# Transformer layer on one core: even tile's scores ahead of the odd tile's transposes in three early steps, with new orders for the downward products, the last output blocks and the second routing product

## The chip, the cores and the metric

The kernel runs on one core of a Trainium2 chip. The metric is the device time of one execution in microseconds (us). A measurement of this kernel tells a change from none at about 0.2%, some 2.3 us.

## The reference

One pre-norm transformer layer over x of 8 batches x 512 tokens x 256 features, all float32:

```python
x = x + attention(layernorm(x))   # rms norm with gamma, 16 heads of 64, softmax(q k^T / 8) v, w_out
x = x + ffn(layernorm(x))         # gelu(x w1 + b1) w2 + b2, 256 -> 1024 -> 256
# the ffn result is scaled by the sum of the two renormalised top router
# probabilities of 8 experts
```

## The kernel before

Every float32 operand of a product is split in two parts, hi (the value rounded to fp32r) and lo (the rest), and a product is three matmuls: hi with hi, lo with hi, hi with lo. ScalarE (ACT) or GpSimd (POOL) writes the hi part and VectorE (DVE) the lo part, from the matmul's result in PSUM. All engines walk lists written out by hand, in the order of the code; semaphores tie them together. TensorE (PE) takes its weight loads and matmuls from one list too.

**Attention.** A tile n is 128 queries of a pair of heads; there are 256 tiles, four to a pair (`NUNIT`). The loop goes over steps -10 to 129, two tiles to a step. PE does in step s: the 64x64 transposes of the probabilities of the odd tile 2s-3 (`transpose_prob`, recorded at L681, 32 in all), the scores of tiles 2s and 2s+1 (`scores`, L642 and L648, six matmuls for each), the transposes of the even tile 2s-2, then projection blocks (`aux`, its products at L615: in steps 3, 5 and 7 the one block of v; in even steps q and k of a coming pair; from step 8 on output blocks too), and in odd steps the weighted values of a pair (`weighted_values`, L696, 16 matmuls). In step 127 the scores of tile 254 already precede the transposes of tile 251.

What is waited for around the change:

- `scores(n)` waits for both exponentials of tile n-2 (`exp`, ACT L980), whose bank it writes.
- `transpose_prob` of the odd tile 2s-3 in an odd step waits until DVE has the lo part of tile 2s-4 (`transposed_lo`, DVE L1204, `s_ptlo`); that of the even tile 2s-2 in an odd step waits for the lo part of the keys projected in the step before (`aux_done` of k, DVE L1204, `nat`).
- `aux` of a block at place 1, as the v block of steps 3, 5 and 7, waits for the first half of the lo part of the odd tile 2s-3: `pe.wait_ge(s_ptlo, 2 * tile + (1 if place == 1 else 2))`.
- DVE does in an odd step: the reciprocal of tile 2s-1, the lo part of the late keys, `transposed_lo(2s-3)` in two halves, `row_max(2s)` (L1288), `transposed_lo(2s-2)`, `row_max(2s+1)`.

**The seam.** Steps 128 and 129 also hold the first four upward products of the feed-forward part (`up`, L615, six matmuls of 512 columns for each). The lo part of the last attention-side input, `input_lo(8)`, is done by DVE at the end of step 127; `up(0, 0)` waits for it. Step 128 has two output blocks of 12 matmuls each, out(30, 0) and out(30, 1).

**Feed-forward.** For each batch c: eight `up` blocks, gelu on ACT (L995), hi part on POOL (L1084), lo part on DVE (L1204), then `down` for four tiles of 128 tokens. In `down`, each of eight slices f of the hidden features is one matmul of 512 columns (hidden hi with both parts of w2, L856, last L860) and one of 256 (hidden lo with w2 hi, L857, last L859), alternating; the last tile of batch 7 is three matmuls of 256 columns a slice. Tile 0 waits for the lo part of each slice (`s_hlo`). In batch 0, after two tiles, come the last two output blocks (`last_outs`, 24 matmuls, waiting for the last pair's attention output from POOL, L1112) and then `route(1)`, the router's product for batch 1 (L824, four matmuls of 512 columns). `up(c, f)` waits for the gelu two blocks before, and that, from the fourth on, for the lo part three blocks before.

Of the kernel before, what the change touches and what calls it, by code (L numbers as in the profile page):

```python
# [31 lines left out]
P = 128  # L32
B, SEQ, D = 8, 512, 256
# [6 lines left out]
FT = FF // P  # L40
# [3 lines left out]
NUNIT = 2 * NHEAD  # L44
# [12 lines left out]
STEPS = NUNIT // 2  # L57
# [4 lines left out]
TAIL_UPS = 4  # L62
# [9 lines left out]

PS_UP = (0, 1)
PS_ROUTER = 2
PS_DOWN = (5, 6, 4, 7)
PS_LAST_OUT = (3, 1)

# [58 lines left out]
def layer_kernel(nc, x, gamma_cols, w_qkv, w_out, router_w, w1, b1_cols, w2, b2_rows, ident, out):  # L136
# [13 lines left out]
    with ExitStack() as ctx:  # L150
# [6 lines left out]
        ps = ctx.enter_context(nc.psum_tensor("ps", [P, 8, 512], F32))  # L157
# [7 lines left out]
        w2_both = wbig_parts[:, :, KT * FF:KT * FF + FT * D].rearrange("p i (k n) -> p k i n", k=FT)  # L165
# [51 lines left out]
        def hidden(part, f):  # L217

            assert (STEPS - 2) % NHALF == 0
            place = 2 * (f % TT)  # L220
            return pT[part][:, 0 if f >= TT else 2, place:place + 2, :].rearrange("p k q -> p (k q)")
# [106 lines left out]
        def down_bank(c, tile):  # L328
            return PS_DOWN[tile]

        def by_parts(c, tile):

            return c < B - 1 or tile < TT - 1
# [276 lines left out]
        def _(pe):  # L610
            def products(dst, stationary, moving, first, last):

                terms = [(0, 0), (1, 0), (0, 1)]
                for n, (i, j) in enumerate(terms):
                    ins = pe.matmul(dst, stationary[i], moving[j], start=first and n == 0,  # L615
                                    stop=last and n == len(terms) - 1)
                return ins
# [211 lines left out]
            def up(c, f):  # L829
                n = c * FT + f  # L830
                if n == 0:
                    wait_x2_split(0)
                    wait_weight_split(pe, 9)
                    pe.wait_ge(s_exp, 2 * NUNIT - 2)
                if n >= 2:
                    pe.wait_ge(s_gelu, n - 1)
                if n == FT + 1:
                    pe.wait_ge(s_added, len(out_tasks))
                for k in range(KT):
                    ins = products(ps[:, PS_UP[n % 2], :], [w[:, k, f * P:(f + 1) * P] for w in w1s],  # L840
                                   [v[c % 2][:, k, :] for v in f_xT], k == 0, k == KT - 1)
                ins.then_inc(s_up, 1)

            def down(c, tile):
                part, t = divmod(tile, 2)
                if c >= 1 and t == 0:
                    pe.wait_ge(s_fo, 2 * (c - 1) + part + 1)
                for f in range(FT):
                    if tile == 0:
                        pe.wait_ge(s_hlo, c * FT + f + 1)  # L850
                    bank = ps[:, down_bank(c, tile), :]
                    tokens = [hidden(i, f)[:, tile * P:(tile + 1) * P] for i in range(2)]
                    if not by_parts(c, tile):
                        ins = products(bank[:, 0:D], tokens, [w[:, f, :] for w in w2s], f == 0, f == FT - 1)
                    elif f < FT - 1:
                        pe.matmul(bank, tokens[0], w2_both[:, f], start=f == 0, stop=False)  # L856
                        pe.matmul(bank[:, 0:D], tokens[1], w2s[0][:, f, :], start=False, stop=False)  # L857
                    else:
                        pe.matmul(bank[:, 0:D], tokens[1], w2s[0][:, f, :], start=False, stop=False)  # L859
                        ins = pe.matmul(bank, tokens[0], w2_both[:, f], start=False, stop=True)  # L860
                if t == 1 or tile == TT - 2 and c == B - 1:
                    ins.then_inc(s_down, 1)

# [1 line left out]
                for n in range(count):  # L865
                    pe.matmul(ps[:, PS_SCORE[1], :], pT[0][:, 0, 0, 0:P], pT[0][:, 0, 0:2, :], start=True, stop=True)

            SCORE_TILES = {1: (4,), 2: (5,), STEPS - 1: (NUNIT - 1,)}

            pe.wait_ge(s_warm, 1)  # L870
            for step in range(FIRST_STEP, LAST_STEP + 1):
                keep_warm(WARM.get(step, 0))
                first, rest = aux_of(step)
                tail = 2 * step - UP_SLOT
                if step == STEPS - 1:
                    scores(2 * step)
                if 0 <= 2 * step - 3 < NUNIT:
                    transpose_prob(2 * step - 3)
                for n in SCORE_TILES.get(step, (2 * step, 2 * step + 1)):
                    if 0 <= n < NUNIT:  # L880
                        scores(n)
                if 0 <= 2 * step - 2 < NUNIT and step != 1:
                    transpose_prob(2 * step - 2)
                if 0 <= tail < TAIL_UPS:
                    up(0, tail)
                for block_of_aux in first:
                    if block_of_aux[1:3] == (2, "out") and first[-1][2] == "k":
                        begin_keys(step, *first[-1])
                    aux(step, *block_of_aux)
                if step == LAST_STEP:  # L890
                    up(0, tail + 1)
                if pair_at(step) is not None:
                    weighted_values(pair_at(step))
                for block_of_aux in rest:
                    aux(step, *block_of_aux)
                    if step == 0 and block_of_aux[2] == "k":
                        scores(2)
                        transpose_prob(0)
                    if step == 0 and block_of_aux[2:] == ("v", 0, 0):
                        scores(3)  # L900
                if 0 <= tail < TAIL_UPS and step < LAST_STEP:
                    up(0, tail + 1)

            route(0)
            for c in range(B):
                for f in range(TAIL_UPS if c == 0 else 0, FT):
                    up(c, f)
                if 1 <= c < B - 1:
                    route(c + 1)
                if c == 0:  # L910
                    wait_weight_split(pe, N_CHUNKS - 1)
                    pe.wait_ge(s_added, added_no(NPAIR // 2 - 2, 1))
                    pe.wait_ge(s_halves, STEPS)
                down(c, 0)
                down(c, 1)
                if c == 0:
                    last_outs()
                    route(1)
                down(c, 2)
                down(c, 3)  # L920

# [245 lines left out]
        def _(dve):  # L1167
# [185 lines left out]
            for step in range(FIRST_STEP, LAST_STEP + 2):  # L1353
                if 0 <= 2 * step - 1 < NUNIT and step < STEPS - 1:
                    row_inverse(2 * step - 1)
                if step == 1:
                    row_max(2)
                    aux_done(*late_blocks(0)[0])
                    row_max(3)
                    row_inverse(2)  # L1360
                    for block_of_aux in late_blocks(0)[1:]:
                        aux_done(*block_of_aux)
                    transposed_lo(0)
                else:
                    for block_of_aux in late_blocks(step - 1):
                        aux_done(*block_of_aux)
                    if 0 <= 2 * step - 1 < NUNIT and step >= STEPS - 1:
                        row_inverse(2 * step - 1)
                    if step == STEPS - 1:
                        row_max(2 * step)  # L1370
                    if 0 <= 2 * step - 3 < NUNIT:
                        transposed_lo(2 * step - 3)
                    if 0 <= 2 * step < NUNIT and step < STEPS - 1:
                        row_max(2 * step)
                    if step % 2 == 0 and 0 <= 2 * step + 1 < NUNIT:
                        row_max(2 * step + 1)
                    if 0 <= 2 * step - 2 < NUNIT:
                        transposed_lo(2 * step - 2)
                    if step % 2 and 0 <= 2 * step + 1 < NUNIT:
                        row_max(2 * step + 1)  # L1380
                    if 0 <= 2 * step < NUNIT:
                        row_inverse(2 * step)
                for block_of_aux in sorted(early_blocks(step), key=lambda block: block[1:3] != (2, "out")):
                    aux_done(*block_of_aux)
                slot_tasks(2 * step)
                slot_tasks(2 * step + 1)
                for block_of_aux in turned_blocks(step):
                    aux_done(*block_of_aux)
                if split_step(step) and split_step(step) < B:
                    input_lo(split_step(step))  # L1390
                if step == STEPS - 1:
                    input_lo(B)

            def turn_logits(c):

# [126 lines left out]
```

## Time and profile before

| | |
|---|---|
| median of 3 runs | 1161.59 us (1160.44 to 1162.55) |
| the profiled execution | 1160.57 us, span 1158.8 us |
| PE busy | 1146.5 us (99%) |
| DVE busy | 1008.1 us (87%) |
| ACT busy | 875.0 us (76%) |
| POOL busy | 664.9 us (57%) |
| granted TensorE clock | 1.00 in every stretch that was read |

Busy time of PE counts modelled ends of matmuls, which overlap the next one. So the time that a matmul takes in a row of them is read from start to start.

### The profile page before, as it was taken

To read this page: it belongs to the slowest core of one execution; us is meant where nothing else is said; L and a number is where in the kernel's file an instruction comes from. 1 tells how busy PE (TensorE), PEld (TensorE's weight loads), DVE (VectorE), ACT (ScalarE), POOL (GpSimd) and SP (SyncE) were. 2 spreads that over 40 slices of the span, in tenths; PEclk is the share of its full clock that TensorE was granted. 3 is DMA by queue.
4 is the path that set the end of the run, shared out by engine and by line. 5 is a ranking of instruction groups with operands and counts; after the bars stand their busy time and mean duration, and the time that the engine had idled before them with its cause. 6 is when DMAs were issued, how large, how long until landed. Compare 5 with 4: busy or idle time off the path is not lost.

```text
span 1158.8 us, 26395 instructions
## 1 busy us (share of the span) xinstructions
PE 1146.5 (99%) x9923; PEld 951.6 (82%) x9923; DVE 1008.1 (87%) x1767; ACT 875.0 (76%) x1896; POOL 664.9 (57%) x827
## 2 busy tenths in 40 slices
PE   9999999999999999999999999999999999999999
PEld 6778888888888888888888888888888877888887
DVE  7889888988888888888888888888988988889985
ACT  6888888888888888888888888888888885334432
POOL 6786566655666565656565656565656586323321
PEclk9999999999999999999999999999999999999999
DMA  4224112311231123112221213121312135334321
GB/s 125 76 78 110 35 34 72 88 33 38 74 92 38 38 74 88 42 38 74 68 63 37 74 55 75 34 72 31 92 33 67 43 110 152 129 112 146 111 75 37
DMA packets 58270, 82.92 MB, mean 72 GB/s; under 512 B 12576, under 2 KB 34592, under 8 KB 58144
## 3 DMA queue, kind: packets, MB, share of 16 engines
q1 hardware_dynamic: 58144, 81.24, 25.4%
q8 instruction: 79, 1.29, 0.5%
q14 instruction: 47, 0.39, 0.1%
HBM read 31.14 MB, written 16.25 MB: 41 GB/s over the span
## 4 chain that ended last, share of the span: by engine, by line
PE 89%; POOL 3%; DVE 1%; issue 1%; ACT 0%; POOLq 0%; ACTq 0%
PE ps L615 34%; PE ps L696 19%; PE ps L681 11%; PE ps L642 10%; PE ps L648 5%; PE ps L856 4%; PE ps L857 2%; POOL prob L1075 1%; PE ps L767 1%; PE ps L766 1%; PE ps L725 1%; PE ps L824 1%; PE ps L860 1%; POOL att_hi_v L1106 1%; POOL attT_lo L1112 0%
## 5 line engine op out<-in xcount | busy, mean ns | idle before, releaser
L1075 POOL TENSOR_SCALAR prob<-prob,rowinv 128x512 f32<-128x512 f32 x512 | 354.3, 704 | 333.1 <-DVE rowinv L1293 333.0
L1204 DVE TENSOR_TENSOR pT_lo<-ps,pT_hi 128x512 fp32r<-128x512 f32 (+1 forms) x384 | 320.5, 863 | 57.1 <-ACT pT_hi L973 55.7
L980 ACT ACTIVATE prob<-ps,negmax 128x512 f32<-128x512 f32 x512 | 347.5, 688 | 16.2 <-DVE negmax L1288 11.7
L1288 DVE TENSOR_REDUCE negmax<-ps 128x2 f32<-128x1024 f32 x256 | 305.8, 1216 | 1.3 <-PE ps L648 1.3
L970 ACT ACTIVATE pT_hi<-ps 128x1024 fp32r<-128x1024 f32 x128 | 131.5, 1027 | 113.4 <-issue 112.1
L681 PEld LDWEIGHTS ps<-identity,prob 64*128 64x128 f32 x4096 | 157.6, 138 | 68.8 <-issue 44.6
L681 PE MATMUL ps<-identity,prob 64*128 64x64 f32 x4096 | 176.0, 225 | 4.0 <-DVE pT_lo L1204 2.1
L642 PE MATMUL ps<-nat 64*128 64x512 f32 x1024 | 170.9, 411 | 1.4 <-ACT prob L980 1.1
L615 PE MATMUL ps<-xT_hi,wbig 128*128 128x512 f32 x514 | 166.7, 405 | 0.2 <-DVE pT_lo L1204 0.2
L973 ACT ACTIVATE pT_hi<-ps 128x512 fp32r<-128x512 f32 x256 | 139.3, 597 | 8.9 <-PE ps L681 0.6
L696 PE MATMUL ps<-pT_hi,vbuf 128*128 128x512 f32 x512 | 138.4, 392 | 0.9 <-DVE pT_lo L1204 0.9
L696 PE MATMUL ps<-pT_lo,vbuf 128*128 128x512 f32 x512 | 137.0, 389 | 0.0
L696 PEld LDWEIGHTS ps<-pT_lo,vbuf 128*128 128x128 f32 x512 | 96.1, 188 | 20.7
L615 PEld LDWEIGHTS ps<-xT_hi,wbig 128*128 128x128 f32 x514 | 91.3, 188 | 20.8 <-issue 0.4
L615 PE MATMUL ps<-wbig,xT_hi 128*128 128x256 f32 x512 | 108.4, 295 | 0.0
L696 PEld LDWEIGHTS ps<-pT_hi,vbuf 128*128 128x128 f32 x512 | 92.1, 189 | 16.8 <-issue 1.0
L980 ACT ACTIVATION_READ_ACCUMULATOR prob<-ps,negmax 128x1 f32 x512 | 104.1, 203 | 0.0
L1084 POOL TENSOR_SCALAR pT_hi<-prob 128x512 fp32r<-128x512 f32 x64 | 49.4, 774 | 92.3 <-ACT prob L995 92.3
L648 PE MATMUL ps<-nat 64*128 64x512 f32 x512 | 101.5, 393 | 0.0
L615 PE MATMUL ps<-xT_lo,wbig 128*128 128x512 f32 x257 | 100.0, 389 | 0.0
L642 PEld LDWEIGHTS ps<-nat 64*128 64x128 f32 x1024 | 87.4, 188 | 14.1 <-ACT prob L980 1.3
L989 ACT ACTIVATE halves_out<-ps 128x512 f32<-128x512 f32 x128 | 76.9, 601 | 13.6 <-PE ps L696 13.6
(118 smaller groups left out, 2061.3 us busy)
## 6 DMA issues: line engine op xcount, KB each, us to landing
att_hi_v<-halves_out SPq DMA_DIRECT2D x128, 128.0 KB, 2.3
att_lo_v<-halves_out SPq DMA_DIRECT2D x128, 128.0 KB, 2.3
blocks_scratch<-xblocks SPq DMA_DIRECT2D x15, 512.0 KB, 2.7
xn<-blocks_scratch SPq DMA_DIRECT2D x60, 128.0 KB, 2.9
xin<-in_x SPq DMA_DIRECT2D x32, 128.0 KB, 3.0
xres<-in_x SPq DMA_DIRECT2D x8, 512.0 KB, 3.6
x_scratch<-xres SPq DMA_DIRECT2D x8, 512.0 KB, 3.5
xin<-x_scratch SPq DMA_DIRECT2D x32, 128.0 KB, 3.2
```

The source lines that it names most:

```text
L615: ins = pe.matmul(dst, stationary[i], moving[j], start=first and n == 0, stop=last and n == len(terms) - 1)
L642: pe.matmul(ps[:, PS_SCORE[n % 2] + h, :], part[rows, q_part, q0:q0 + P], part[rows, k_part, :], start=q_part == QH, stop=False)
L648: pe.matmul(ps[:, PS_SCORE[n % 2] + h, :], part[rows, QH, q0:q0 + P], part[rows, KL, :], start=False, stop=True).then_inc(s_score, 1)
L681: ins = pe.transpose(ps[:, bank + r, a * DH:(a + 1) * DH], prob[rows, n % NPROB, a * P:(a + 1) * P], identity[rows, rows])
L696: ins = pe.matmul(ps[:, value_bank(pair, h), :], vbuf[:, quad % 2, k, pair % 2 * 2 + h, :], pT[part][:, halves_of(pair)[0], h * TT + k, :] ...
L970: act.activation(even_tile(n)[0], two_bank_blocks(tile_banks(n)), ACT.Copy).then_inc(s_pthi, 2)
L973: act.activation(odd_tiles(n)[r][0], bank_blocks(tile_banks(n) + r), ACT.Copy).then_inc(s_pthi, 1)
L980: act.activation(prob[:, n % NPROB, j * SEQ:(j + 1) * SEQ], ps[:, PS_SCORE[n % 2] + j, :], ACT.Exp, bias=negmax[:, n % 4, j:j + 1], accum_ ...
L989: act.activation(halves_out[:, h, :], ps[:, value_bank(pair, h), :], ACT.Copy).then_inc(s_halves, 1)
L1075: return pool.tensor_scalar(dst, src, scalar, 1.0, ALU.mult, ALU.mult)
L1204: return dve.tensor_tensor(dst, full, hi, ALU.subtract)
L1288: dve.tensor_reduce(negmax[:, n % 4, :], ps[:, PS_SCORE[n % 2]:PS_SCORE[n % 2] + 2, :], AX.X, ALU.max, negate=True).then_inc(s_max, 1)
```

## The change

Five things are moved; no instruction of computation is added or removed.

1. In steps 3, 5 and 7 (as in 127 before) PE does `scores(2s)` ahead of the transposes of tile 2s-3, and DVE does `row_max(2s)` ahead of `transposed_lo(2s-3)`.
2. In `down` by parts, the seven 512-column matmuls of slices 0 to 6 come first, then the eight of 256 columns, then the 512-column one of slice 7. Tile 0 waits for the hi parts with `s_hhi` and for the lo parts only at the second group.
3. In step 128 the output blocks precede `up(0, 0)`.
4. `input_lo(8)` goes from the end of step 127 to step 128, behind `transposed_lo(253)`.
5. In batch 0, `route(1)` precedes `last_outs()`.

```diff
+SCORES_FIRST = (3, 5, 7, STEPS - 1)
...
-                for f in range(FT):
-                    if tile == 0:
-                        pe.wait_ge(s_hlo, c * FT + f + 1)
...
-                    elif f < FT - 1:
-                        pe.matmul(bank, tokens[0], w2_both[:, f], start=f == 0, stop=False)
-                        pe.matmul(bank[:, 0:D], tokens[1], w2s[0][:, f, :], start=False, stop=False)
-                    else:
-                        pe.matmul(bank[:, 0:D], tokens[1], w2s[0][:, f, :], start=False, stop=False)
-                        ins = pe.matmul(bank, tokens[0], w2_both[:, f], start=False, stop=True)
+                if by_parts(c, tile):
+                    for f in range(FT - 1):
+                        if tile == 0:
+                            pe.wait_ge(s_hhi, c * FT + f + 1)
+                        pe.matmul(bank, tokens[0][f], w2_both[:, f], start=f == 0, stop=False)
+                    for f in range(FT):
+                        if tile == 0:
+                            pe.wait_ge(s_hlo, c * FT + f + 1)
+                        pe.matmul(bank[:, 0:D], tokens[1][f], w2s[0][:, f, :], start=False, stop=False)
+                    ins = pe.matmul(bank, tokens[0][FT - 1], w2_both[:, FT - 1], start=False, stop=True)
...
-                if step == STEPS - 1:
+                if step in SCORES_FIRST:
                     scores(2 * step)
...
-                if 0 <= tail < TAIL_UPS:
-                    up(0, tail)
                 for block_of_aux in first:
...
+                if 0 <= tail < TAIL_UPS:
+                    up(0, tail)
...
+                    route(1)
                     last_outs()
-                    route(1)
...
-                    if step == STEPS - 1:
+                    if step in SCORES_FIRST:
                         row_max(2 * step)
                     if 0 <= 2 * step - 3 < NUNIT:
                         transposed_lo(2 * step - 3)
-                    if 0 <= 2 * step < NUNIT and step < STEPS - 1:
+                    if step == STEPS:
+                        input_lo(B)
+                    if 0 <= 2 * step < NUNIT and step not in SCORES_FIRST:
                         row_max(2 * step)
...
-                if step == STEPS - 1:
-                    input_lo(B)
```

## Rows read from the trace of the kernel before

**Rows 1.** The page: busy time of an engine; the chain that ended last

```profile
PE 1146.5 (99%) x9923; PEld 951.6 (82%) x9923; DVE 1008.1 (87%) x1767; ACT 875.0 (76%) x1896; POOL 664.9 (57%) x827
...
PE 89%; POOL 3%; DVE 1%; issue 1%; ACT 0%; POOLq 0%; ACTq 0%
```

**Rows 2.** PE's waits, whole span: total us, times, longest us

```profile
PE ps L681 <- DVE pT_lo L1204: 2.1, 3, 1.0
...
PE ps L615 <- POOL attT_lo L1112: 1.0, 1, 1.0
```

**Rows 3.** Table by stretches, 200 to 400 us: busy us, clock, DMA

```profile
200.00:400.00 200.00, 200.00 (x1889) 166.73 (x1888) 176.02 (x280) 168.08 (x379) 119.25 (x152) 1.00 0.23 59
```

**Rows 4.** Timeline of PE, step 3: start us, us, instruction, idle before

```profile
29.04 0.39 PE L615 MATMUL ps<-xT_lo,wbig 128*128 128x512 f32 x1
30.38 0.71 PE L681 MATMUL ps<-identity,prob 64*128 64x64 f32 x16 [0.96 <-DVE pT_lo L1204]
30.91 0.71 PE L642 MATMUL ps<-nat 64*128 64x512 f32 x4
...
31.69 0.62 PE L642 MATMUL ps<-nat 64*128 64x512 f32 x4
...
32.65 0.71 PE L681 MATMUL ps<-identity,prob 64*128 64x64 f32 x16
33.29 0.39 PE L615 MATMUL ps<-wbig,xT_hi 128*128 128x256 f32 x1
```

**Rows 5.** Waits of all engines, 20 to 62 us

```profile
DVE pT_lo L1204 <- ACT pT_hi L973: 1.9, 3, 1.0
PEld ps L681 <- DVE nat L1204: 1.6, 3, 0.5
...
PEld ps L615 <- DVE pT_lo L1204: 0.3, 1, 0.3
```

**Rows 6.** Timeline of DVE, step 3

```profile
31.90 0.69 DVE L1204 TENSOR_TENSOR nat<-ps,nat 128x512 fp32r<-128x512 f32 x1 [0.33 <-ACT nat L949]
32.51 1.28 DVE L1204 TENSOR_TENSOR pT_lo<-ps,pT_hi 128x512 fp32r<-128x512 f32 x2
33.70 1.22 DVE L1288 TENSOR_REDUCE negmax<-ps 128x2 f32<-128x1024 f32 x1
34.83 1.22 DVE L1204 TENSOR_TENSOR pT_lo<-ps,pT_hi 128x1024 fp32r<-128x1024 f32 x1
```

**Rows 7.** Timeline of PE in batch 3: upward blocks, then four downward tiles

```profile
1041.47 11.05 PE L615 MATMUL ps<-nat,wbig 128*128 128x512 f32 x48
1052.36 0.40 PE L824 MATMUL ps<-xT_hi,rw_parts 128*16 128x512 f32 x1
...
1053.27 0.39 PE L856 MATMUL ps<-wbig,pT_hi 128*128 128x512 f32 x1
...
1064.54 0.62 PE L615 MATMUL ps<-xT_hi,wbig 128*128 128x512 f32 x2
```

**Rows 8.** Timeline of PE in step 128

```profile
958.45 0.73 PE L615 MATMUL ps<-xT_hi,wbig 128*128 128x512 f32 x2
...
959.94 0.28 PE L615 MATMUL ps<-wout_hi,attT_hi 128*128 128x256 f32 x1
...
962.82 0.63 PE L615 MATMUL ps<-xT_hi,wbig 128*128 128x512 f32 x2
```

**Rows 9.** Timeline of DVE in steps 127 and 128

```profile
955.16 1.71 DVE L1204 TENSOR_TENSOR xT_lo<-xn,xT_hi 128x512 fp32r<-128x512 f32 x2
...
957.71 1.29 DVE L1204 TENSOR_TENSOR pT_lo<-ps,pT_hi 128x512 fp32r<-128x512 f32 x2 [0.77 <-ACT pT_hi L973]
```

**Rows 10.** Timeline of PE, batches 0 and 1

```profile
985.06 0.36 PE L615 MATMUL ps<-wout_hi,attT_hi 128*128 128x256 f32 x1 [0.98 <-POOL attT_lo L1112]
...
988.01 1.10 PE L824 MATMUL ps<-nat,rw_parts 128*16 128x512 f32 x4
...
1001.82 4.55 PE L615 MATMUL ps<-nat,wbig 128*128 128x512 f32 x18 [0.25 <-ACT prob L995]
```

**Rows 11.** Timeline of DVE and of ACT, batches 0 and 1

```profile
980.50 1.22 DVE L1204 TENSOR_TENSOR nat<-xn,nat 128x1024 fp32r<-128x1024 f32 x1
...
1000.31 1.89 DVE L1204 TENSOR_TENSOR pT_lo<-prob,pT_hi 128x512 fp32r<-128x512 f32 x3
...
1001.08 0.69 ACT L995 ACTIVATE prob<-ps,b_sb 128x512 f32<-128x512 f32 x1 [1.50 <-DVE pT_lo L1204]
```

More of the change, by code:

```diff
@@ L847, in down @@
                     pe.wait_ge(s_fo, 2 * (c - 1) + part + 1)
-                for f in range(FT):
-                    if tile == 0:
-                        pe.wait_ge(s_hlo, c * FT + f + 1)
[L851 to L854, printed above, removed]
-                    elif f < FT - 1:
-                        pe.matmul(bank, tokens[0], w2_both[:, f], start=f == 0, stop=False)
-                        pe.matmul(bank[:, 0:D], tokens[1], w2s[0][:, f, :], start=False, stop=False)
-                    else:
-                        pe.matmul(bank[:, 0:D], tokens[1], w2s[0][:, f, :], start=False, stop=False)
-                        ins = pe.matmul(bank, tokens[0], w2_both[:, f], start=False, stop=True)
+                bank = ps[:, down_bank(c, tile), :]
+                tokens = [[hidden(i, f)[:, tile * P:(tile + 1) * P] for f in range(FT)] for i in range(2)]
+                if by_parts(c, tile):
[8 more added lines that the diff above has]
+                    ins = pe.matmul(bank, tokens[0][FT - 1], w2_both[:, FT - 1], start=False, stop=True)
+                else:
+                    for f in range(FT):
+                        ins = products(bank[:, 0:D], [v[f] for v in tokens], [w[:, f, :] for w in w2s],
+                                       f == 0, f == FT - 1)
                 if t == 1 or tile == TT - 2 and c == B - 1:
@@ L866, in keep_warm @@
                     pe.matmul(ps[:, PS_SCORE[1], :], pT[0][:, 0, 0, 0:P], pT[0][:, 0, 0:2, :], start=True, stop=True)
-            SCORE_TILES = {1: (4,), 2: (5,), STEPS - 1: (NUNIT - 1,)}
+            SCORE_TILES = {1: (4,), 2: (5,)}
+            SCORE_TILES.update({step: (2 * step + 1,) for step in SCORES_FIRST})
             pe.wait_ge(s_warm, 1)
```

## The prediction

> **What bounds the kernel now.** I read the page first: PE is busy 99% of the span and carries 89% of the chain that ended last [rows 1]. The table by stretches shows how hard this holds in the long middle: 200.00 of 200 us, at the full granted clock [rows 3]. So time can be won only where PE waits, or where its matmuls stand closer together, and anything that makes PE wait in front of the middle is never won back. The list of PE's waits names the places [rows 2]: three waits of 2.1 us in all of the transposes for DVE's lo parts, and one of 1.0 us for the last attention output. The timelines put the three at the odd tile's transposes of steps 3, 5 and 7 and the single one at the last output blocks. These are the places that the change touches, so each needs the question: what releases the work behind the stall?
>
> **Steps 3, 5 and 7, on PE.** In step 3 the last matmul before the stall starts at 29.04 and the transposes of tile 3 start at 30.38 [rows 4]. The scores of tile 6 take 0.78 us (30.91 to 31.69) and now fall in this hole; what they wait for, the exponentials of tile 4, is past by then, and if it were not, only this hole would be filled less. But the next thing that PE does after both scores is the even tile's transposes, at 32.65, and the view of waits shows that their weight loads wait for DVE's lo part of the late keys, in all three steps, 0.5 us each [rows 5]. That part starts on DVE at 31.90, released by ACT [rows 6], and nothing in the change moves it: ACT's order is unchanged, and it goes through the exponentials of tile 5, which were already under way. So the even transposes stay at 32.65 and the hole filled at 30.38 opens again just in front of them. PE's part of the edit is worth 0, where its face value is the 2.1 us of the three waits.
>
> **Steps 3, 5 and 7, on DVE.** DVE's order there was: lo part of the keys (31.90), the two halves of tile 3's lo part (from 32.51), maximum of tile 6 (33.70), lo part of tile 4 (34.83) [rows 6]. Now the maximum comes ahead of the halves. It takes 34.83 - 33.70 = 1.13 us from start to start, so the first half starts at 32.51 + 1.13 = 33.64. DVE's own idle (0.33 us and an earlier one) lies before the keys' lo part and so cannot take the maximum in. Who waits for the first half? The v block, which is the odd step's block at place 1. It started at 33.29 [rows 4], 0.78 us after the half's start at 32.51, and in one of the three steps the view already shows a weight load of L615 waiting for that very lo part, 0.3 us [rows 5]. There is no slack: the v block starts at 33.64 + 0.78 = 34.42, that is 1.13 us later. The whole of PE's list behind it (v block, weighted values, the transposes of tile 5) moves by as much. The lo part of tile 4 stays at its time, since the same three operations stand ahead of it.
>
> Is the delay given back before the next such step? The trace has a stall at tile 7's transposes in step 5, but it is no cushion: DVE's lo part there waits for ACT's hi part (the row of 1.9 us, three times) [rows 5], which waits for tile 5's transposes on PE, and these moved too. The chain from one v block to the next is rigid, so step 5 adds its own 1.13 us and step 7 a third. From step 8 on PE has no idle at all, so nothing returns. Sum: 3 x 1.13 = +3.39 us. Bounds: below, +3 x (1.13 - 0.3) = +2.5, if the 0.3 us that the view shows for that wait [rows 5] were slack in each step and not a wait; above, +3 x 1.22 = +3.7, the maximum's full duration. I take 3.4, since the row of step 3 has the two starts themselves.
>
> **Downward products.** Four tiles take 1064.54 - 1053.27 = 11.27 us, 2.82 us each [rows 7], for eight matmuls of 512 and eight of 256 columns that alternate: 352 ns a pair. Unmixed, 48 matmuls of 512 columns take 1052.36 - 1041.47 = 10.89 us, 227 ns each [rows 7], and 24 of 256 columns 962.82 - 959.94 = 2.88 us, 120 ns each [rows 8], each with a weight load of its own, as here. A tile in groups would take 8 x 227 + 8 x 120 = 2.776 us; with some 8 ns for each of the edges that stay (first, and last 512-column matmul) 2.79. That is 0.03 us a tile. Bounds: 0 and 2.82 - 2.776 = 0.04. It counts where PE sets the pace: the four tiles of batches 1 to 6 and three of batch 7, 27 tiles, 27 x 0.033 = -0.9 us (0 to -1.1). Those of batch 0 are absorbed, as follows. The waits that tile 0 now has on hi parts come free before those on lo parts did, and the last lo product stands at 7 x 227 + 7 x 120 = 2.43 us in the tile where it stood at 7 x 352 = 2.46, so the wait on the last slice isn't worsened by more than 0.03 us; 0.
>
> The Trainium skill, TensorE: Matmul & The Clock Gate, section Back-to-back issue gap, gives N/2.4 + 2.5 ns for N columns whatever stands beside it; by that rule the order of the sixteen would change nothing and this term would be 0 (the second rival). The trace's 227 against the page's 216 speaks for using the rows.
>
> **Step 128.** The output blocks (24 matmuls, 2.88 us) and `up(0, 0)` change places. PE starts at 958.45 [rows 8]; the first output block needs the first half of tile 253's lo part, which starts at 957.71 [rows 9], and 957.71 + 0.78 = 958.49: 0.04 us late, taken as 0. `up(0, 0)` then starts at 958.45 + 2.88 = 961.33 and needs `input_lo(8)`, which follows DVE's pair at 957.71 + 1.29 = 959.00 and takes up to 1.71 us: 960.71, hidden with 0.6 us to spare. DVE's freed place at 955.16 lets POOL normalise tile 254 sooner, but the half at 957.71 holds PE at 958.5 anyway. Bounds: -0.1, +0.5 (if the lo part of tile 254, pushed behind, disturbed the end of the step). I take 0.
>
> **The second routing product.** `route(1)`, four matmuls at 988.01 [rows 10], is 4 x 227 ns = 0.9 us, and now fills the wait of 0.98 us that ends at 985.06 [rows 10]; its input (DVE, 980.50 + 1.22 = 981.72 [rows 11]) is there. So PE reaches the upward blocks of batch 1 about 0.9 us sooner. But there, at 1001.82, PE waits for a gelu [rows 10], which at 1001.08 waited 1.50 us for DVE's lo part, the first of three in a row at 1000.31 [rows 11]. That row has no idle before it: DVE comes to it straight out of its list (routing, statistics, residual, the first outputs), which the change neither shortens nor starts earlier. PE's 0.9 us turns into a longer wait before 1001.82. Value 0; bounds 0 and -0.94.
>
> **Sum** against the profiled execution (1160.57 us, span 1158.8): +3.39 - 0.9 = +2.5, so 1163.1. The median of the runs shown lies 1.0 above that execution: 1161.59 + 2.5 = **1164.1 us**.
>
> **The rivals.**
>
> - *The forecast*: 1164.1, own range 1163.2 to 1165.0. Chance 0.63.
> - *The grouped downward products pay nothing* (alternation wasn't what cost the 8 ns, or the two-part operand of w2 costs it in any order): 1161.6 + 3.4 = 1165.0. For it: that operand stands in no unmixed row. Against it: the alternating pairs are the only ones at 352 ns. 0.15.
> - *The routing product's 0.9 us lasts*, since DVE's stretch shortens when its inputs come sooner: 1163.2. Against it: DVE has no idle there to lose. 0.10.
> - *The maximum is free* (the v block has hidden slack over 1.13 us): the first term is 0, 1161.6 - 0.9 = 1160.7. Against it: the v block starts 0.78 us after the half that it waits for. 0.07.
> - *Faster*: DVE does the maximum in its idle before the keys' lo part and that part is done earlier as well, so both PE's stall and the reopened hole go: -2.1 - 0.9 = -3.0, 1158.6. It decides only if the even transposes of step 3 come before 32.65 and the v block before 33.29; the keys' hi part on ACT speaks against it. 0.05.
>
> **How the numbers follow.** Slower by over 0.2% (about what a measurement of this kernel tells from no change) is above 1163.9. The forecast is just above it: of its 0.63 I give 0.39 to slower and 0.24 to same; with the second case slower has 0.54; same has 0.24 + 0.10 + 0.07 = 0.41; faster 0.05. The range from 1162.5 to 1165.5 holds the first three cases less their tails.
>
> **What would show it.** Right: no idle at the odd transposes of steps 3, 5 and 7, and in its place PE (and its weight loads) waiting some 1.1 us at L615 for DVE's pT_lo, three times; every step from 9 on 3.4 us later; a downward tile of 2.79 us; the wait for attT_lo gone and the wait for the gelu before batch 1's sixth upward block over 1 us. Wrong: the v block of step 3 at 33.3, downward tiles still at 2.82, or a PE that passes 1001.8 earlier than the shift of the steps before allows.

## The result, and the profile after

The changed kernel takes 1164.29 us (median of 8 runs, 1163.23 to 1167.28) where the kernel before takes 1161.61 (8 runs, 1160.44 to 1162.55). The ratio is 1.0029 with a 95% interval of 1.0020 to 1.0039: slower by 2.7 us by the medians, 3.4 by the ratio. Three executions alone show a mean granted clock below 1.00: two of these eight (1166.95 and 1167.28 us, both 0.997), without which the difference of the means is 2.5 us, and one of the kernel "with all" in the first relief for VectorE, below (1375.06 us, 0.753), which is not in its ratio. The forecast was 1164.1. The profiled execution took 1163.88 us, span 1162.1, which is 3.3 more than that of before.

The page, its busy times and its chain of what ended last, against [rows 1]:

```profile
PE 1147.4 (99%) x9923; PEld 951.4 (82%) x9923; DVE 1006.4 (87%) x1767; ACT 875.3 (75%) x1896; POOL 666.9 (57%) x827
...
PE 90%; DVE 5%; ACT 2%; issue 1%; POOL 1%; SPq 0%; DMA 0%; ACTq 0%; DVEq 0%; POOLq 0%
```

The counts of instructions are those of before. In the chain DVE's share went from 1% to 5% and POOL's from 3% to 1%. PE's waits over the whole span (total us, times, longest), against [rows 2]:

```profile
PE ps L616 <- DVE pT_lo L1209: 3.7, 5, 1.0
PE ps L643 <- ACT prob L985: 2.0, 5, 1.1
...
PE ps L616 <- ACT prob L1000: 1.1, 2, 0.7
...
PE ps L682 <- DVE nat L1209: 0.8, 3, 0.3
```

In the kernel before, the waits for the exponentials were a single one:

```profile
PE ps L642 <- ACT prob L980: 1.1, 1, 1.1
```

The waits of the transposes (L682 here) for DVE's pT_lo are gone, 2.1 us in three. In their place stand three waits of 1.0 us of the v block (L616) for lo parts, and small waits for the exponentials (L643, four new ones with 0.9 us in all) and for the keys' lo part (L682 for nat). Also gone is the 1.0 us wait for attT_lo; the waits for gelus (L1000) grew from 0.25 [rows 10] to 1.1 us. The timeline of PE in step 3, against [rows 4]:

```profile
29.63 0.73 PE L643 MATMUL ps<-nat 64*128 64x512 f32 x4 [0.20 <-ACT prob L985]
...
30.44 0.69 PE L682 MATMUL ps<-identity,prob 64*128 64x64 f32 x16
31.46 0.73 PE L643 MATMUL ps<-nat 64*128 64x512 f32 x4 [0.33 <-ACT prob L985]
...
32.67 0.71 PE L682 MATMUL ps<-identity,prob 64*128 64x64 f32 x16 [0.25 <-DVE nat L1209]
34.40 0.39 PE L616 MATMUL ps<-wbig,xT_hi 128*128 128x256 f32 x1 [1.01 <-DVE pT_lo L1209]
```

The hole before the odd transposes is filled. The next ones open before the second scores (31.46) and before the even transposes (32.67, within 0.02 us of the 32.65 of before), and the v block starts at 34.40 instead of 33.29. On DVE, against [rows 6]:

```profile
31.93 0.69 DVE L1209 TENSOR_TENSOR nat<-ps,nat 128x512 fp32r<-128x512 f32 x1 [0.32 <-ACT nat L954]
32.53 1.22 DVE L1293 TENSOR_REDUCE negmax<-ps 128x2 f32<-128x1024 f32 x1
33.67 2.41 DVE L1209 TENSOR_TENSOR pT_lo<-ps,pT_hi 128x512 fp32r<-128x512 f32 x3
```

The maximum takes the place of the first half of the lo part, which now starts at 33.67 (three operations merged: two halves of tile 3, then tile 4). From there to the v block are 0.73 us; the forecast had 33.64 and 34.42. The v blocks of steps 5, 7 and 9 on PE, in the changed kernel:

```profile
49.82 0.39 PE L616 MATMUL ps<-wbig,xT_hi 128*128 128x256 f32 x1 [1.02 <-DVE pT_lo L1209]
...
65.22 0.38 PE L616 MATMUL ps<-wbig,xT_hi 128*128 128x256 f32 x1 [1.01 <-DVE pT_lo L1209]
...
80.06 0.39 PE L616 MATMUL ps<-wbig,xT_hi 128*128 128x256 f32 x1
```

The same v blocks in the kernel before:

```profile
47.63 0.38 PE L615 MATMUL ps<-wbig,xT_hi 128*128 128x256 f32 x1
...
61.97 0.38 PE L615 MATMUL ps<-wbig,xT_hi 128*128 128x256 f32 x1
...
76.81 0.39 PE L615 MATMUL ps<-wbig,xT_hi 128*128 128x256 f32 x1
```

So, with that of step 3, they are late by 1.11, 2.19, 3.25 and again 3.25 us: about 1.1 us a step, three times, and then constant up to step 11. (0.03 us of it was there before step 3.)

The later edits, on PE from step 128 on, against [rows 8, 10]:

```profile
961.48 0.39 PE L616 MATMUL ps<-wout_hi,attT_hi 128*128 128x256 f32 x1 [0.51 <-DVE pT_lo L1209]
...
986.83 1.09 PE L825 MATMUL ps<-nat,rw_parts 128*16 128x512 f32 x4
988.05 0.36 PE L616 MATMUL ps<-wout_hi,attT_hi 128*128 128x256 f32 x1
...
996.59 2.90 PE L616 MATMUL ps<-nat,wbig 128*128 128x512 f32 x12
1000.16 4.37 PE L616 MATMUL ps<-nat,wbig 128*128 128x512 f32 x18 [0.67 <-ACT prob L1000]
1004.99 4.54 PE L616 MATMUL ps<-nat,wbig 128*128 128x512 f32 x18 [0.46 <-ACT prob L1000]
```

The routing product (L825) fills the wait before the last output blocks. PE then stalls twice in batch 1's upward blocks instead of once, and starts the sixth at 1004.99, 3.17 us after the 1001.82 of before. The four downward tiles of batch 2, the upward blocks behind them and the next routing product, against [rows 7]:

```profile
1033.29 1.75 PE L855 MATMUL ps<-wbig,pT_hi 128*128 128x512 f32 x7
1034.88 1.12 PE L859 MATMUL ps<-wbig,pT_lo 128*128 128x256 f32 x8
1035.83 0.40 PE L860 MATMUL ps<-wbig,pT_hi 128*128 128x512 f32 x1
...
1044.44 11.12 PE L616 MATMUL ps<-nat,wbig 128*128 128x512 f32 x48
1055.39 0.40 PE L825 MATMUL ps<-xT_hi,rw_parts 128*16 128x512 f32 x1
```

Four tiles take 1044.44 - 1033.29 = 11.15 us (before 11.27), so 2.79 a tile. But the 48 upward matmuls behind them take 1055.39 - 1044.44 = 10.95 (before 10.89).

**How the runs are compared.** There is one trace of each kernel, and even where the kernels are alike the traces differ by more than the small terms asked about: by up to 0.5 us at the start of step 3, and again in the waits at 114 to 118 us. So beside each run's time and ratio I give the stretch that its edit touches, start to start within one trace.

### The profile page after: what moved, and what is told of

The parts are those of the page before. It is cut to its first block, busy times and chain, and to the rows that moved or that the text cites. A ratio compares the mean times of both kernels' runs of the same rounds, so it can differ in the third digit from the quotient of the medians.

```text
span 1162.1 us, 26395 instructions
## 1 busy us (share of the span) xinstructions
PE 1147.4 (99%) x9923; PEld 951.4 (82%) x9923; DVE 1006.4 (87%) x1767; ACT 875.3 (75%) x1896; POOL 666.9 (57%) x827
## 4 chain that ended last, share of the span: by engine, by line
PE 90%; DVE 5%; ACT 2%; issue 1%; POOL 1%; SPq 0%; DMA 0%; ACTq 0%; DVEq 0%; POOLq 0%
PE ps L616 34%; PE ps L697 19%; PE ps L682 12%; PE ps L643 10%; PE ps L649 5%; PE ps L855 3%; PE ps L859 2%; PE ps L768 1%; PE ps L767 1%; PE ps L726 1%; DVE pT_lo L1209 1%; DVE negmax L1293 1%; ACT prob L985 1%; DVE f_o L1453 1%; PE ps L825 0%
## 5 line engine op out<-in xcount | busy, mean ns | idle before, releaser
L682 PEld LDWEIGHTS ps<-identity,prob 64*128 64x128 f32 x4096 | 157.7, 138 | 65.8 <-issue 44.3
L682 PE MATMUL ps<-identity,prob 64*128 64x64 f32 x4096 | 175.6, 225 | 1.8 <-DVE nat L1209 0.8
L643 PE MATMUL ps<-nat 64*128 64x512 f32 x1024 | 171.3, 412 | 2.3 <-ACT prob L985 2.0
L616 PE MATMUL ps<-xT_hi,wbig 128*128 128x512 f32 x514 | 166.9, 406 | 0.2 <-DVE pT_lo L1209 0.2
L616 PE MATMUL ps<-wbig,xT_hi 128*128 128x256 f32 x512 | 108.4, 295 | 3.0 <-DVE pT_lo L1209 3.0
L616 PEld LDWEIGHTS ps<-xT_hi,wbig 128*128 128x128 f32 x514 | 91.1, 188 | 21.7 <-ACT prob L1000 1.1
L1089 POOL TENSOR_SCALAR pT_hi<-prob 128x512 fp32r<-128x512 f32 x64 | 52.5, 824 | 90.6 <-ACT prob L1000 90.6
L643 PEld LDWEIGHTS ps<-nat 64*128 64x128 f32 x1024 | 87.1, 188 | 16.3 <-ACT prob L985 3.8
L616 PE MATMUL ps<-xT_lo,wbig 128*128 128x512 f32 x257 | 100.1, 389 | 0.0
```

The source lines that it names most:

```text
L643: pe.matmul(ps[:, PS_SCORE[n % 2] + h, :], part[rows, q_part, q0:q0 + P], part[rows, k_part, :], start=q_part == QH, stop=False)
L682: ins = pe.transpose(ps[:, bank + r, a * DH:(a + 1) * DH], prob[rows, n % NPROB, a * P:(a + 1) * P], identity[rows, rows])
```

## The experiments

### TensorE's half of the swap alone

```diff
--- before
+SCORES_FIRST = (3, 5, 7, STEPS - 1)
...
-                if step == STEPS - 1:
+                if step in SCORES_FIRST:
                     scores(2 * step)
```

> Before, with the scores of the even tile ahead of the odd tile's transposes on TensorE alone in steps 3, 5 and 7; VectorE keeps its order. My theory (the even transposes wait for the lo part of the late keys, the v block for the odd tile's lo part, and neither moves): the three v blocks start within 0.1 us of 33.29, 47.63 and 61.97, the time is that of before, 0.0 (-0.2 to +0.2). Rival (the swap on TensorE itself delays the odd tile's transposes, their hi parts and with them the v block): v blocks late by 0.3 us or more each, time +1 us. Rival (the swap pays what the waits showed): -2.1 us.

Measured: 1161.38 us against 1161.78, ratio 0.9999 (0.9990 to 1.0008). The timeline of PE in step 3 of this kernel:

```profile
30.63 0.69 PE L682 MATMUL ps<-identity,prob 64*128 64x64 f32 x16
...
32.88 0.71 PE L682 MATMUL ps<-identity,prob 64*128 64x64 f32 x16 [0.25 <-DVE nat L1206]
33.52 0.39 PE L616 MATMUL ps<-wbig,xT_hi 128*128 128x256 f32 x1
```

This execution is 0.22 us late from its start on; less that, the even transposes stand at 32.66 and the v block at 33.30. In steps 5, 7 and 9 it is late by the same 0.22. The waits of the odd transposes, 2.1 us in the kernel before, are gone from the list, and the time is that of before. The edit moved the wait from the odd transposes to the second scores and the even transposes. The forecast had the even transposes; the wait before the second scores it had not named.

### VectorE's half alone

```diff
--- before
+SCORES_FIRST = (3, 5, 7, STEPS - 1)
...
-                    if step == STEPS - 1:
+                    if step in SCORES_FIRST:
                         row_max(2 * step)
...
-                    if 0 <= 2 * step < NUNIT and step < STEPS - 1:
+                    if 0 <= 2 * step < NUNIT and step not in SCORES_FIRST:
                         row_max(2 * step)
```

> Before, with the even tile's maximum ahead of the odd tile's lo part on VectorE alone in steps 3, 5 and 7; TensorE keeps its order. My theory: VectorE's maximum now stands in front of the half that the v block waits for, so each v block is 1.1 us late and the sum is +3.3 us (+2.9 to +3.6), the whole of what the changed kernel lost in these steps. It may be somewhat more, if the scores that the maximum waits for come after 32.5 us. Rival (only both swaps together cost it, since TensorE's scores stand in the way): under +1 us.

Measured: 1165.02 us against 1161.78, ratio 1.0026 (1.0016 to 1.0036). PE's waits in this kernel:

```profile
PE ps L616 <- DVE pT_lo L1205: 3.0, 3, 1.0
PE ps L682 <- DVE pT_lo L1205: 2.1, 3, 1.0
```

Both sets of waits are there: the old ones of the transposes, since PE's order is the old one, and the new ones of the v block. Against before, the v block ahead of step 3 stands at -0.11 us, those of steps 3, 5 and 7 at +0.98, +2.08 and +3.17, and that of step 9 at +3.17: a drift of 3.28 us in all. This half alone is the whole loss.

### The maximum first in two more steps

```diff
--- the kernel of the last experiment (VectorE's half alone)
-SCORES_FIRST = (3, 5, 7, STEPS - 1)
+SCORES_FIRST = (3, 5, 7, 9, 11, STEPS - 1)
```

> Before, with the maximum ahead of the odd tile's lo part on VectorE alone, in steps 3, 5, 7, 9 and 11. My theory prices each step by where the first half starts in the kernel before: in steps 9 and 11 it starts 1.08 us ahead of the v block (75.73 and 90.56 against 76.81 and 91.64), 0.30 more than the 0.78 that the v block needs, so the 1.13 us of the maximum costs 0.83 in each: +3.3 + 1.7 = +5.0 us against before. Rival (TensorE's list from step 8 on has slack enough to take it): +3.3 us. Rival (every step costs the same): +5.5 us.

Measured: 1165.76 us against 1161.66, ratio 1.0037 (1.0024 to 1.0049). The v blocks of steps 9 and 11 in the timeline of PE of this kernel:

```profile
81.11 0.39 PE L616 MATMUL ps<-wbig,xT_hi 128*128 128x256 f32 x1 [0.76 <-DVE pT_lo L1205]
...
96.77 0.39 PE L616 MATMUL ps<-wbig,xT_hi 128*128 128x256 f32 x1 [0.76 <-DVE pT_lo L1205]
```

The timeline of DVE in this kernel, ahead of the first of them (the maximum, then the lo parts):

```profile
79.23 1.22 DVE L1289 TENSOR_REDUCE negmax<-ps 128x2 f32<-128x1024 f32 x1
80.37 2.44 DVE L1205 TENSOR_TENSOR pT_lo<-ps,pT_hi 128x512 fp32r<-128x512 f32 x3
```

Against before the v blocks of steps 7, 9, 11 and 13 are late by 3.47, 4.30, 5.13 and 5.13 us. Each of the two further steps costs 0.83 us, the number worked out from the starts in the trace of before. This trace is 0.22 us late from its start on, so steps 3 to 7 made 3.25 us and all five 4.9. By the medians the kernel lost 4.1, by the ratio 4.3, with the interval reaching from 2.8 to 5.7, so it is the v blocks and not the time that decide against the rival of +3.3. The pricing (where the first half starts, and the 0.78 us from there to the v block) came out right to 0.05 us a step, with 0.30 us of slack and with next to none.

### The grouped downward products alone

```diff
--- before
-                for f in range(FT):
...
+                    for f in range(FT - 1):
...
+                        pe.matmul(bank, tokens[0][f], w2_both[:, f], start=f == 0, stop=False)
+                    for f in range(FT):
...
+                        pe.matmul(bank[:, 0:D], tokens[1][f], w2s[0][:, f, :], start=False, stop=False)
+                    ins = pe.matmul(bank, tokens[0][FT - 1], w2_both[:, FT - 1], start=False, stop=True)
```

> Before, with the grouped downward products alone. The forecast's term: a tile of 2.79 us instead of 2.82 and -0.9 us in all. What the changed kernel's trace suggests instead: tiles of 2.79 us, but the upward blocks of batches 2 to 6 wait for gelus that wait for VectorE's lo part, giving back 0.07 us or more a batch, so -0.6 to 0.0 us. Rival (the grouping pays in full and the loss in the changed kernel's feed-forward part came from the other edits): -0.9 us and upward stages of 10.89 us as before.

Measured: 1161.55 us against 1161.78, ratio 0.9997 (0.9988 to 1.0006). Four tiles of batch 2 and the upward blocks behind them, on PE in this kernel:

```profile
1031.18 1.75 PE L854 MATMUL ps<-wbig,pT_hi 128*128 128x512 f32 x7
...
1042.34 11.12 PE L615 MATMUL ps<-nat,wbig 128*128 128x512 f32 x48
1053.29 0.40 PE L824 MATMUL ps<-xT_hi,rw_parts 128*16 128x512 f32 x1
```

Tiles 11.16 us, upward stage 10.95: 0.11 won and 0.06 given back, as in the changed kernel. So the giving back belongs to this edit. What ACT waited for from 1022 us on, in this kernel (in the kernel before, the same view has 30.6 us in 42 waits for PE's blocks, and no wait for pT_lo):

```profile
ACT prob L998 <- PE ps L615: 23.8, 33, 2.7
ACT prob L998 <- DVE pT_lo L1207: 6.0, 9, 1.3
```

When the downward tiles get shorter, PE comes to the upward blocks sooner, while DVE's list sets when the first lo parts are ready; the gelus that reuse their buffers wait, and PE waits for the gelus. In batches 2 to 5 the first lo part starts 5.05 us after PE's first upward matmul; in the kernel before it is 4.84.

In batch 6 the upward stage took 11.44 us in this execution and 11.45 in that of the changed kernel, 0.5 more than in batches 2 to 5. That isn't the edit alone. DVE's list there waits for the router's logits, which come by DMA. DVE ahead of batch 6's upward blocks, in the changed kernel and in the kernel before:

```profile
1112.48 0.19 DVE L1409 TENSOR_TENSOR r_logit<-r_parts 128x32 f32<-128x32 f32 x1 [0.86 <-DMA r_parts<-r_blocks]
...
1109.17 0.19 DVE L1404 TENSOR_TENSOR r_logit<-r_parts 128x32 f32<-128x32 f32 x1 [0.61 <-DMA r_parts<-r_blocks]
```

In batches 2 to 5 this wait is 0.54 us in each of the three kernels; in batch 6 it is 0.86 in the changed kernel and 1.10 in this one. With the same tiles and a wait of 0.71 us, the changed kernel without the edit of steps 3, 5 and 7 (below) has 10.95 us in batch 6 too; with the old tiles and a wait of 1.00 us, the kernel of the next experiment has 10.93. So the 0.5 us came where late logits met the shorter tiles; these traces are all that speaks for it. From the first downward tile of batch 1 to that of batch 7, this trace is 0.14 us longer than that of before, the changed kernel's 0.12 longer, and the changed kernel's without steps 3, 5 and 7 is 0.40 shorter.

### The routing product first, alone

```diff
--- before
-                    last_outs()
                     route(1)
+                    last_outs()
```

> Before, with the second routing product ahead of the last output blocks alone. My theory: TensorE reaches batch 1's upward blocks 0.9 us sooner and waits there for the same gelu, so that it passes at 1001.8 us as before: 0.0 us (-0.1 to +0.1). Rival (the gain lasts): -0.9 us.

Measured: 1161.64 us against 1161.78, ratio 0.9996 (0.9987 to 1.0006). PE in batch 1's upward blocks in this kernel:

```profile
994.45 2.88 PE L615 MATMUL ps<-nat,wbig 128*128 128x512 f32 x12
998.00 4.37 PE L615 MATMUL ps<-nat,wbig 128*128 128x512 f32 x18 [0.66 <-ACT prob L995]
1002.83 2.49 PE L615 MATMUL ps<-nat,wbig 128*128 128x512 f32 x9 [0.46 <-ACT prob L995]
```

At the start of the downward stage of batch 0 this execution is 0.80 us behind that of before, at batch 1's upward blocks 0.13 ahead (994.45 against 994.58): the 0.93 us is won. At the sixth block it is 1.01 behind again. All of the gain goes into two waits for gelus, and with it 0.2 us more. From the first downward tile of batch 0 to that of batch 1 the changed kernel and the changed kernel without steps 3, 5 and 7 lose the same 0.2 (0.18 and 0.19); no run here says why.

### The edits of steps 127 and 128 alone

```diff
--- before, PE
                 for block_of_aux in first:
...
+                if 0 <= tail < TAIL_UPS:
+                    up(0, tail)
--- before, DVE
+                    if step == STEPS:
+                        input_lo(B)
...
-                if step == STEPS - 1:
-                    input_lo(B)
```

> Before, with the edits of steps 127 and 128 alone (output blocks ahead of the first upward block, input_lo later). The forecast: 0.0 (-0.1 to +0.5). My theory now, from the changed kernel's trace: the first output block waits 0.1 us past where the upward block stood, and nothing gives it back before 1001.8 us, where TensorE waits for VectorE's list, which starts from TensorE too: +0.1 us (0.0 to +0.2). Rival (it starts the upward stage's inputs sooner and pays): -0.3 us.

Measured: 1161.13 us against 1161.60, ratio 1.0000 (0.9991 to 1.0008). From the last v block to the first downward tile this trace is 0.04 us shorter than before's, the changed kernel's 0.06. That is neither the loss of 0.1 us that I expected here nor a gain that can be told from nothing.

### The changed kernel without the edit of steps 3, 5 and 7

```diff
--- after
-SCORES_FIRST = (3, 5, 7, STEPS - 1)
+SCORES_FIRST = (STEPS - 1,)
```

> The changed kernel with the edit of steps 3, 5 and 7 undone on both engines (step 127 as in both kernels). My theory: the loss of 3.3 us goes, what stays is the grouped downward products, the seam and the routing product, worth -0.5 us in all against before (-0.9 to +0.1), so about 1161.2 where before has 1161.7. Rival (the other edits cost something that the single runs don't show, since the changed kernel's feed-forward part was 0.15 us longer than before): +0.2 to +0.5 us.

Measured: 1160.82 us (11 runs) against 1161.60 (33 runs), ratio 0.9993 (0.9985 to 1.0002). The loss is gone. What stays is a small gain at most, whose interval includes none. The v blocks of steps 3 to 9 all stand +0.06 to +0.08 us from those of before, as the one ahead of step 3 does (+0.07).

### Relief for VectorE, first try

The wait for gelus goes back to DVE: between a batch's two finishes it computes the router's weights of the next batch, some 1.9 us, ahead of the first lo part. Here these weights, and the sum of residual and bias, are moved ahead of the shifted logits.

```diff
--- the kernel of the last experiment (all), and before (relief only)
-                if c >= 1:
-                    base(c)
...
+                if c >= 1:
+                    routing_weight(c)
+                    base(c)
                 if c + 1 < B:
                     routing_shift(c + 1)
                 finish(c, 0)
-                if c + 1 < B:
-                    routing_weight(c + 1)
                 finish(c, 1)
```

> The same, and on VectorE the router's weights of batch c+1 and the sum of residual and bias are moved behind the logits' transposes, off the stretch between the two finishes of a batch. My theory (that stretch holds back the first lo part of the next batch, and with it the gelu that TensorE waits for, so it ate both the routing product's 0.9 us and half of the grouping's): now both are paid, with the wait of 0.44 us before batch 1's sixth block: -0.9 - 0.9 - 0.4 = -2.2 us against before (-1.6 to -2.6), near 1159.5. Rival (VectorE is short of time as a whole, and moving its work moves the wait): -0.5 us, as without it.

> Before, with that move on VectorE alone. My theory: the only wait that it can take away in the feed-forward part is the 0.44 us before batch 1's sixth upward block: -0.4 us (-0.6 to 0.0). Rival (the move is what pays in the run with all): -2 us here too.

Measured: with all, 1161.56 us against 1161.60, ratio 0.9999 (0.9990 to 1.0008); alone, 1162.38, ratio 1.0007 (0.9998 to 1.0016). (One of the eleven executions with all took 1375.06 us.) Both expectations missed. In the run alone, the timeline of DVE in batch 1:

```profile
1009.46 1.41 DVE L1180 BATCH_NORM_STATS2 ln_stats<-xin 128x6 f32<-128x256 f32 x4 [1.50 <-DMA xin<-x_scratch]
```

And the timeline of PE in batch 2 of the same run:

```profile
1021.64 0.74 PE L615 MATMUL ps<-xT_hi,wbig 128*128 128x512 f32 x2 [1.03 <-ACT prob L995]
```

The wait at the sixth block of batch 1 went, and the next batch paid for it. With the residual's sum moved away DVE comes to the statistics before their input has landed, and that sum and the weights then stand ahead of the shifted logits (the first operation on the logits starts at 1018.69, in the kernel before at 1016.87). ACT does the router's exponentials (1019.36) and a table load of 1.28 us ahead of the first gelu (1020.90), so the gelus come late. My design moved the wait, which says nothing against the theory but doesn't support it either.

### Relief for VectorE, second try

```diff
--- after without steps 3, 5, 7 (first), and before (second)
                     hidden_lo(c * FT + f)
+                    if f == 1 and c >= 1:
+                        routing_weight(c)
...
                 finish(c, 0)
-                if c + 1 < B:
-                    routing_weight(c + 1)
                 finish(c, 1)
```

> The changed kernel without the edit of steps 3, 5 and 7, and on VectorE only the router's weights of the next batch moved, from between the two finishes of a batch to behind the first two lo parts of the next one; the sum of residual and bias stays where it was, so that the router's exponentials keep their time. My theory: VectorE's first lo part comes 1.9 us sooner, the wait before batch 1's sixth upward block goes (0.4 us), the grouped tiles pay in full (-0.8), and of the routing product's 0.9 us only 0.3 is kept, since the first gelu of batch 1 still waits for the router's exponentials on ScalarE: -1.5 us against before (-1.0 to -2.0). Rival (TensorE's time in this part is held by something else): -0.5 us as without it.

> Before, with that move of the router's weights alone. My theory: it takes away only the wait before batch 1's sixth upward block: -0.4 us (-0.7 to -0.2). Rival: -1.5 us or 0.0.

> The first kernel of this call with the routing product back behind the last output blocks. My theory: without the gelu's wait on VectorE the routing product's place is worth 0.3 us, so this is 0.3 us slower than the first: -1.2 us against before. Rival (the place is worth its 0.9 us): -0.6 us; (it is worth nothing): -1.5 us.

Measured, each against 1161.66 us of before:

| kernel | median, us | ratio (95%) |
|---|---|---|
| all but steps 3, 5, 7, weights later | 1160.22 | 0.9987 (0.9978 to 0.9996) |
| weights later alone | 1160.91 | 0.9994 (0.9985 to 1.0003) |
| the first, routing product in its old place | 1159.82 | 0.9986 (0.9977 to 0.9995) |

PE in batch 1 of the third:

```profile
994.70 10.77 PE L616 MATMUL ps<-nat,wbig 128*128 128x512 f32 x45
1005.30 0.40 PE L825 MATMUL ps<-xT_hi,rw_parts 128*16 128x512 f32 x1
```

The view names no wait in those 45 matmuls, and the stage takes 11.30 us (1005.30 less 994.00), before 11.63. It does not run at the full pace yet: in the later batches it takes 10.90, so some 0.4 us of short delays are left that the view doesn't name. From the first downward tile of batch 0 to that of batch 1 the trace is 0.37 us shorter than before's, with the weights alone moved 0.22. In batches 2 to 6 the upward stage takes 10.90 us (before 10.89, changed kernel 10.95), so the grouping's 0.12 us a batch is kept but for 0.01. With the routing product first, the same stretch of batch 0 is 0.47 us shorter, only 0.10 more, and the medians don't favour it: I had expected the kernel without it to be 0.3 us slower, and it measured 0.4 faster. PE in batch 1 of the first shows why:

```profile
994.54 2.90 PE L616 MATMUL ps<-nat,wbig 128*128 128x512 f32 x12
998.12 8.71 PE L616 MATMUL ps<-nat,wbig 128*128 128x512 f32 x36 [0.67 <-ACT prob L1000]
```

The third block still waits for the batch's first gelu, which on ACT stands behind the router's exponentials (995.84) and a table load of 1.28 us (996.08). The kernels of the first and third rows are faster than before with intervals clear of one, though by less than the 0.2% named at the start; the third is the best that was run, 1.8 us below before and 4.5 below the changed kernel by the medians.

## Why the prediction was right

- **TensorE's swap worth 0**: right. Alone it measured 0.9999, with the even transposes and the v block where they were. One step of the reasoning was incomplete: the scores too had to wait for exponentials in the new place, 0.20 us before the first ones and 0.33 before the second (step 3 of the changed kernel). It cost nothing, since the even transposes waited for the keys' part after that.
- **VectorE's swap +1.13 us a step, rigid from step to step, nothing given back**: right, and shown by doing it alone (3.28 us of drift, ratio 1.0026). In the changed kernel the three steps cost 1.11, 1.08 and 1.06 us, 3.25 in all against 3.39. The term is too large by what the first half was allowed: the v block follows its start by 0.73 us where it had to wait for it, not by 0.78, so there were 0.05 us of slack a step and not none. The two further steps cost 0.83 each, as priced.
- **Downward tiles 2.79 instead of 2.82 us**: the mechanism was right and the term mis-sized. A batch's four tiles win 0.12 us, six batches 0.72; the three tiles of batch 7 took 2.80 already and win nothing. Of the 0.72, the upward stages gave back 0.06 a batch, and 0.5 at once in batch 6 of the profiled execution, where the router's logits came late by DMA as well. The sentence that failed is that in batches 1 to 6 "PE sets the pace": before, PE and DVE's list met there with hardly anything to spare, and 0.12 us was more than that. The profile of before had no PE wait there and so did not show how near the other list was. With VectorE relieved the term came in at 0.64, without that at 0.40 at the best, and at nothing in the changed kernel's profiled execution. The second rival (the grouping pays nothing) had the size nearly right and the reason wrong. The prediction also took a page for a rule that the order can't matter. The Trainium skill, TensorE: Matmul & The Clock Gate, section Back-to-back issue gap, gives N/2.4 + 2.5 ns by the number of columns alone, as the gap of an isolated matmul, and has no word on the order in a stream. In these tiles the order did matter, 11.27 us against 11.15.
- **Step 128: 0**: right; the stretch got 0.04 to 0.06 us shorter.
- **Routing product 0**: right, with a wait more than forecast. The 0.93 us was won and lost in front of two gelus, not one: 0.46 us before the sixth block, for the gelu held by DVE's lo part (the forecast had over 1 us), and ahead of it 0.67 before the third, for the first gelu behind the router's exponentials. The rival in which it lasts fell even with VectorE relieved (0.10 us).
- The sum was +2.5; measured +2.7 by the medians, +3.4 by the ratio, and +3.3 between the two profiled executions. That the last is so near the 3.25 of the three steps is a coincidence of small parts: the delay against before is 3.25 us up to step 11, 3.02 in step 13, 2.97 at the first downward tile, 3.15 at that of batch 1 and 3.27 at that of batch 7. The drop at step 13 is of the size by which other traces differ there. So "from step 8 on PE has no idle at all" does not hold for the whole span, and what held is that the delay wasn't given back by more than 0.3 us. That the median came within 0.2 us of the forecast is partly luck: the first term was 0.14 too large, the second worth about 1.0 less than forecast in that trace, and the reference point, 1.0 us above the profiled execution, rested on three executions.
- **Faster**: fell. The even transposes came at 32.67, not sooner.

**Left open:** whether the late keys' parts could be brought forward on ScalarE so that the early scores pay at all. No kernel here tried it.

## What to carry to other kernels

When an engine stalls, filling the stall is worth nothing unless what the engine waits for next moves too: look one wait further before pricing it at its length. When two operations of an in-order engine change places, ask who waits for the one that is now second, and price it from the starts in the trace; a delay ahead of a stage without idle is paid in full, as the 3.25 us here. A small gain on the busiest engine lasts only if the lists of the engines that it waits for are ahead by as much, and a view without waits doesn't say by how much they are.

## What was not expected

Matmuls of 512 and 256 columns that alternate took more than the same ones in groups, at a granted clock of 1.00 and with the same weight loads: four tiles 11.27 us against 11.15, which is some 4 ns for each pair of the two. In the last batch the same alternation cost nothing (its tiles took 2.80 us before and after); no run here says why.

The executions differ from each other in certain places. At 110 to 120 us DVE's lo part of the next batch's input waits for POOL's hi part, 0.76 us in the execution of before, 1.59 in that of the first kernel with the weights later, though the two kernels are the same up to there. Another such place is the wait for the router's logits in batch 6, 0.54 to 1.10 us in the traces here. The timeline of DVE in the kernel before:

```profile
111.63 2.27 DVE L1205 SCALAR_TENSOR_TENSOR xT_lo<-xn,gain,xT_hi 128x512 fp32r<-128x512 f32 x2 [0.76 <-POOL xT_hi L1075]
```

And in that of the first kernel with the weights later:

```profile
112.58 2.27 DVE L1210 SCALAR_TENSOR_TENSOR xT_lo<-xn,gain,xT_hi 128x512 fp32r<-128x512 f32 x2 [1.59 <-POOL xT_hi L1080]
```

That execution came out of this place 0.80 us later than before's, and all its later gains brought its end only 0.15 us ahead, while its median is 1.4 us faster. A single profile's end is no measure of a change of this size.
